# The logit products of a batch, issued before the step's context products instead of behind the first layer's products

## What is computed

```python
x = x + _L0_xcond_ref(ctx_1024, _layernorm(x), _lenS2, condB_pt, W_a, W_c)   # local attention over a window, tanh
...
h = gelu(ctx @ w1 + b1)                        # first layer, ctx = [layernorm(x), slot mean]
route_logits = (h @ w2 + b2) / (abs(tau) + 0.1)  # the logits: 64 per row
topk_vals, topk_idx = top_k(route_logits, 8)
alpha = (one_hot(topk_idx, 64) * softmax(topk_vals)[..., None]).sum(-2)
slot_input = einsum('bts,btd->bsd', alpha, x)  # the slot sums of a batch
...                                            # GRU update of 64 slots, slot attention, layernorm
out = einsum('bts,bsd->btd', alpha, slot_values) @ wo + bo
x = x + out
```

## Time and profile before

| what | value |
|---|---|
| times of three runs | 348.9, 349.7, 349.93 us; median 349.7 us |
| the profiled execution | 349.35 us, of it 347.4 us between the first and the last instruction |
| TensorE, matmul records | 329.5 us busy, 95% of the span |
| VectorE, ScalarE, GpSimd | 261.0, 198.8 and 209.2 us busy (75%, 57%, 60%) |
| granted TensorE clock | 0.993 of full speed on the mean |
| chain that ended last | PE 56%, DVE 14%, POOL 7%, issue 7%, ACT 7%, DMA 6% |

### The profile page before, as it was taken

One profiled execution on the slowest core, in us unless ns is written; L12 is line 12 of the kernel. 1 busy time (PEld: TensorE's weight loads), 2 busy tenths in 40 slices (PEclk: granted clock), 3 DMA queues, 4 the chain that ended last, 5 costly groups with the idle time before them and its releaser, 6 DMA issues.

```text
span 347.4 us, 7118 instructions
## 1 busy us (share of the span) xinstructions
PE 329.5 (95%) x2320; PEld 284.3 (82%) x2320; DVE 261.0 (75%) x749; ACT 198.8 (57%) x406; POOL 209.2 (60%) x353
## 2 busy tenths in 40 slices
PE   8899998999998999999999999999999999999981
PEld 6597856999898998898989989986889886877750
DVE  5989898675789798788787877766953766477873
ACT  3367225567768759668569677666754336313521
POOL 5600156879687776974976884746575335235782
PEclk9999999999999999999999999999999999999997
DMA  7999975232323232232241200008900000000797
GB/s 271 261 321 353 343 216 182 93 114 69 109 74 114 71 98 88 62 119 65 62 122 62 86 9 2 0 0 271 314 1 2 1 2 0 0 0 3 291 393 283
DMA packets 40934, 42.79 MB, mean 123 GB/s; under 512 B 3245, under 2 KB 32045, under 8 KB 40898
## 3 DMA queue, kind: packets, MB, share of 16 engines
q1 hardware_dynamic: 38944, 40.19, 35.4%
q10 hardware_dynamic: 1666, 1.49, 1.3%
q0 software_dynamic: 288, 0.66, 0.7%
HBM read 32.18 MB, written 8.39 MB: 117 GB/s over the span
## 4 chain that ended last, share of the span: by engine, by line
PE 56%; DVE 14%; POOL 7%; issue 7%; ACT 7%; DMA 6%; SPq 1%; DVEq 0%; ACTq 0%; POOLq 0%
PE psum L456 13%; PE psum L457 12%; PE psum L458 12%; PE psum L1741 4%; PE psum L2003 3%; DMA xT<-in_xT 3%; POOL X L604 3%; PE psum L1770 3%; DMA encw<-in_enc,rowi 2%; ACT th L1320 2%; DVE st L971 2%; PE psum L1721 2%; PE psum L1805 1%; DVE xhT_lo L958 1%; PE psum L1952 1%
## 5 line engine op out<-in xcount | busy, mean ns | idle before, releaser
L456 PE MATMUL psum<-GW_hi,hT_hi 128*128 128x292 f32 (+1 forms) x256 | 78.6, 307 | 0.0
L458 PE MATMUL psum<-GW_lo,hT_hi 128*128 128x292 f32 (+1 forms) x256 | 74.0, 289 | 0.0
L457 PE MATMUL psum<-GW_hi,hT_lo 128*128 128x292 f32 (+1 forms) x256 | 73.9, 289 | 0.0
L604 POOL TENSOR_TENSOR X<-X,th 128x512 f32<-128x512 f32 x32 | 38.3, 1196 | 29.0 <-ACT th L1320 28.5
L456 PEld LDWEIGHTS psum<-GW_hi,hT_hi 128*128 128x128 f32 x256 | 48.5, 189 | 1.8 <-issue 1.4
L457 PEld LDWEIGHTS psum<-GW_hi,hT_lo 128*128 128x128 f32 x256 | 48.4, 189 | 0.0
L458 PEld LDWEIGHTS psum<-GW_lo,hT_hi 128*128 128x128 f32 x256 | 48.1, 188 | 0.0
L599 POOL TENSOR_TENSOR hT_lo<-xT,hT_hi 128x512 fp32r<-128x512 f32 x30 | 39.1, 1304 | 2.0 <-DVE stack L982 2.0
L971 DVE BATCH_NORM_STATS2 st<-X 128x6 f32<-128x512 f32 x32 | 22.2, 693 | 22.6 <-POOL X L604 22.6
L456 PE MATMUL psum<-xhT_hi,w_hi 128*128 128x256 f32 x128 | 38.0, 297 | 1.1 <-issue 1.0
L457 PE MATMUL psum<-xhT_hi,w_lo 128*128 128x256 f32 x128 | 36.1, 282 | 0.0
(11 more groups left out here) (316 smaller groups left out, 919.0 us busy)
## 6 DMA issues: line engine op xcount, KB each, us to landing
xT<-in_xT SPq DMA_DIRECT2D x32, 256.0 KB, 2.8
X<-in_x SPq DMA_DIRECT2D x32, 256.0 KB, 3.5
out<-ost SPq DMA_DIRECT2D x32, 256.0 KB, 2.8
WhhT<-in_WhhT SPq DMA_DIRECT2D x1, 3072.0 KB, 12.9
WihT<-in_WihT SPq DMA_DIRECT2D x4, 768.0 KB, 6.8
Wo<-in_wo ACTq DMA_DIRECT2D x4, 256.0 KB, 4.4
WvpT<-in_WvpT SPq DMA_DIRECT2D x4, 256.0 KB, 5.2
WaT<-in_WaT SPq DMA_DIRECT2D x1, 1024.0 KB, 12.1
```

The lines of the kernel that those rows point to most:

```text
L456: pe.matmul(out, w_hi, m_hi, start=start, stop=False)
L457: pe.matmul(out, w_lo, m_hi, start=False, stop=False)
L458: return pe.matmul(out, w_hi, m_lo, start=False, stop=stop)
L604: pool.tensor_tensor(tile_x(r), tile_x(r), halves(th[:, :]), ALU.add).then_inc(S("x2"), 1)
```

## The change

The six calls of `logits` in TensorE's loop move from behind `first_layer` to ahead of `context`. Nothing else is touched; the calls for batches 6 and 7 stay.

```diff
@@ -1815,6 +1815,9 @@
                 right_half(s)
             if s == BIAS_STEP:
                 bias_row()
+            for b in range(NB):
+                if LOGIT_STEP[b] == s:
+                    logits(b)
             if live(s) and s:
                 context(s - 1)
             if s in TOPK_STEP:
@@ -1833,9 +1836,6 @@
                     turn_alpha(b, trX, b)
             first_layer(s, 0)
             first_layer(s, 1)
-            for b in range(NB):
-                if LOGIT_STEP[b] == s:
-                    logits(b)
             extras(s)
             if live(s - 2):
                 turn_rows(s - 2, len([b for b in range(NB) if SLOT_STEP[b] + TPB <= s]),
```

## The result

Twenty-two timed runs of each kernel give a median of 349.76 us with the change and 349.12 us before; the ratio is 1.0031, with a 95% interval of 1.002 to 1.0043. So the kernel is a little slower, by 0.7 to 1.5 us, at the edge of what a measurement can tell. A second set of runs of the same changed kernel gave 1.0017 (0.9996 to 1.0037). The profiled execution took 349.37 us, its span is 347.2 us.

The account below looks back on a forecast made before the run. TensorE is 95% busy, but ScalarE's tanh loop starts the steps behind the first logits. Terms 0 + 0 + 0.22 + 0 + 0.02 + 0.05 = 0.29, say +0.3 us, on 349.35 or 349.7: 349.8 us, range 348.7 to 351.0.

Parts of the forecast that it names:

- Step 8: Logits fill TensorE's gap ahead of the context; score of tile 9 0.44 us earlier, tile 10 unchanged: worth 0.
- Step 12: Logits fill the 0.55 us gap ahead of the context, but the score of tile 14 stays at 120.41: worth 0.
- Step 16: No gap; logits delay the slot transposes, so ScalarE's copy and tanh come later: costs 0.22 us, bounds 0 to 0.35.
- Step 20: ScalarE copies 1.90 us behind the right half, so the 1.83 us fit: costs 0, with 0.07 to spare.
- Step 24: ScalarE copies 1.81 us behind the right half, against 1.83 us needed: costs 0.02 us.
- Step 28: TensorE's own queue is the bound, with one more change of kind: costs 0.05 us, between 0 and 0.1.
- The rival with the longer block: Logits take longer ahead of a context than charged; 0.3 us more each gives 350.75 us; chance 0.13.
- x: Time the logits block takes beyond the charge; cost 0.22 + 4x us, slower by 0.3% from 0.21 us.
- TensorE alone decides: Rival: about 1.04 us gained at each of steps 8 and 12, 347.6 us; chance 0.08 together with its half, 348.75.

Follow-up runs that it names:

- the kernel with L1026 moved: Kernel before, with VectorE's operation L1026 moved ahead of the row statistics of the same step; ratio 0.9951, again 0.9978.
- the one with the tanh first: Changed kernel, with ScalarE's tanh put ahead of its copy of the turned slots; ratio to the kernel before 1.0016.

## Why the prediction came out as it did

The forecast was no measurable change, with a loss of 0.3 us in sum. The traces show a loss of 0.43 us, in the places that the prediction named; the timed runs say 0.7 to 1.5. That the forecast of 349.8 us lies next to the measured median of 349.76 is luck: it was reached from 349.35 and 349.7 with +0.3, and the larger set has the kernel before at 349.12 and the change at +0.64.

- *Step 8, worth 0.* Right, by its own numbers: the score of tile 9 was to start at 90.45 and starts at 90.47 on the clock of before; that of tile 10 stays, 96.55 against 96.52.
- *Step 12, worth 0.* Right: 0.02 us at tile 14, and with these two steps alone 0.00.
- *Step 16, 0.22 us.* The mechanism is right, its size a little short. The end of the right half (0.09 ahead of the first logits record, at 135.66) to ScalarE's copy at 137.53 is 1.87 us, forecast 1.83: the context takes 0.35, not 0.31, behind the logits. On the clock of before the copy starts 0.27 us later instead of 0.22; the copy, the tanh and GpSimd's sum add 0.04 on the way to `alT`, which makes the 0.31 at tile 18. The 0.05 that TensorE's own queue lost by tile 17 is not part of it, since TensorE waits for `alT` there.
- *Step 20, 0.* Right (0.01).
- *Step 24, 0.02.* It measured 0.10, between tiles 24 and 26. The copy starts 0.07 us later than the loss up to there explains (1.87 us behind the right half against 1.81, just outside the 0.05 that the prediction allowed), and the chain to `alT` adds 0.03. TensorE's own queue loses 0.04 by tile 25, but at the turned rows of step 25 it waits for `alT`, 0.11 us instead of 0.05.
- *Step 28, 0.05.* Measured 0.01 to 0.03.
- *The rival with the longer block* was decided by x = 0.21. x came out at 0.04.
- *TensorE alone decides* is refuted by the kernel with steps 8 and 12 alone: not 1.0 us each but 0.00. The rule of the Trainium skill that the prediction cites (Perfetto Trace Analysis, Optimization Strategy) says where to look, and the gap was there and could be filled. What a filled gap is worth it does not say; that it counts in full was the prediction's reading, and the runs show 0.00, since the work behind the gap had a second thing to wait for.

What was mis-sized is the way back from the plain fp32 products to the rounded ones, 0.07 us in the prediction. It was read at 87.87 to 88.06, where the first layer stands behind the context; both are rounded, so that row shows no change of kind but a product behind a wait. The trace of the kernel before has the right place: the slot sums (L1741) are plain fp32 products, and the first product behind them takes 0.23 us to the next one instead of 0.12.

```profile
129.17 1.96 PE L1741 MATMUL psum<-X,A 128*64 128x258 f32 x16
131.06 0.39 PE L456 MATMUL psum<-xhT_hi,w_hi 128*128 128x256 f32 x1
131.29 0.28 PE L457 MATMUL psum<-xhT_hi,w_lo 128*128 128x256 f32 x1
```

With 0.11 for the way back the context takes 0.35 us, which is what the changed kernel shows (136.76 to 137.11), and the sum for step 16 is the measured 1.87 us. The loss exceeds the forecast by this 0.04 us at both steps, 16 and 24, and by the 0.04 and 0.03 that the chain from the copy to `alT` adds, for which the prediction had nothing; step 28 cost less than it charged.

What stays open: the 0.43 us are a ratio of 1.0012, and the first, larger set of timed runs excludes that narrowly (1.002 at least). No stretch of the two traces of each kernel shows the rest. The timed runs themselves give a hint. Their length goes with their mean granted clock: of the 22 runs of the changed kernel the six at 0.991 or less average 351.0 us and the sixteen at 0.992 or more 349.7. Where the clocks of both kernels are on record, runs at 0.992 or more can be compared alone: 349.55 us for the changed kernel (nine runs) and 349.69 for the kernel with the moves from step 16 on (eleven) against 349.09 for the kernel before (26 runs of the same set). That is 0.5 and 0.6 us, each with a standard error of 0.2 to 0.3, which agrees with 0.43. For the first set the clocks of the kernel before are not on record, so that its 0.64 us have this cause is argued, not shown.

## What to carry to other kernels

A gap on the busiest engine is worth only as much as the next thing that its queue waits for is early. Before filling one, look one and two steps further: if the start there lies a semaphore's time (0.14 to 0.15 us here) behind another engine's end, the gain is gone by then. And look at what is queued behind the place where the filling goes: here two small transposes, 0.4 us of work, carried nearly the whole loss (0.31 us at step 16 and 0.10 at step 24, of 0.43), because another engine's copy of them stands in front of the operation that starts the next step.

## What the runs showed beside it

- The loop repeats within 0.03 us at the starts of tiles 2 to 31 in the kernel before and in the changed one (two traces each), while over all thirteen traces the stretch ahead of it varies by up to 4 us. In the kernel with L1026 moved the two traces agree to 0.04 us from tile 4 to tile 25 and lie 0.2 us apart from tile 26 on (-1.36 and -1.16). The traces show where they part: at step 23 VectorE's L1003, the same instruction on the same data, takes 0.72 us in the first and 1.14 in the second. In both it ends 0.28 us behind GpSimd's sum L604, which started 0.76 us ahead of it in the first and 0.34 in the second. Behind it ScalarE's copy of the slots at step 24 is 0.31 us later, `alT` 0.20, and so is tile 26. First trace, then second:

```profile
183.33 1.20 POOL L604 TENSOR_TENSOR X<-X,th 128x512 f32<-128x512 f32 x1
184.09 0.72 DVE L1003 SCALAR_TENSOR_TENSOR kept<-kept,lsub 128x256 f32<-128x256 f32 x1
...
182.81 1.20 POOL L604 TENSOR_TENSOR X<-X,th 128x512 f32<-128x512 f32 x1
183.15 1.14 DVE L1003 SCALAR_TENSOR_TENSOR kept<-kept,lsub 128x256 f32<-128x256 f32 x1
```

  With no GpSimd operation beside it L1003 takes 0.41 to 0.43 us; at step 23 it takes 1.11 to 1.18 in all traces but two, the first one here (0.72) and the one with the tanh first (0.58).
- Of GpSimd's and VectorE's operations on 512 columns the one that started later was the longer one. In the kernel before with L1026 moved, the sum L604 starts 0.33 to 0.48 us before L1026 ends and takes 1.38 to 1.52 us at the four steps, against 1.18 to 1.19 at the same steps before; L1026 takes 0.74. In the kernel before L1026 starts 0.39 us before GpSimd's L599 ends (91.53 + 1.29 against 92.44) and takes 0.94. So the move of L1026 also shortened L1026 and lengthened L604; the gains above are the sum of both.
- Between rounded and plain fp32 products TensorE lost 0.09 us on the way into the logits, and 0.11 in the context behind them (0.35 against 0.24). The first product behind a wait takes about as much more: in the context of step 8 of the kernel before, which stands behind 0.57 us of idle time, it is 0.22 us from the first product to the second.
